# Weighing the values of two key tiles at a time, at the end of every second step, in a causal attention kernel

## The chip, the cores and the metric

The kernel runs on one core of one Trainium2 chip, in one launch. The metric is the device time in microseconds, the median of a few executions; lower is better. One further execution was taken by the hardware profiler, and all rows below come from that one.

## The reference, cut to what matters

The input `x` is 2 sequences of 2048 tokens with 256 channels. It is layer-normalised, then goes through a 16-head attention (16 channels a head) and, beside it, through a small gated feed-forward part; both results are added to `x`.

```python
att = jnp.einsum('bhqd,bhkd->bhqk', q, k) / np.sqrt(HEAD_DIM)
att = jnp.where(causal, att, 0.0)          # masked scores are 0, not -inf
att = jax.nn.softmax(att, axis=-1)
out = jnp.einsum('bhqk,bhkd->bhqd', att, v)
```

The masked scores are 0 and not minus infinity, so keys after the query keep a weight of exp(0 - row maximum) and their values have to be added in. The row maximum has to be known before the exponentials are taken.

## The kernel before, in words

A first stage (`stage_tokens`, the first 270 us or so) normalises the tokens, makes the projections, splits queries and keys into three bf16 parts each and writes them to HBM, together with the values and the feed-forward result. The second stage (`stage_attention`) is what the change touches.

**Groups, units, steps.** The 32 (sequence, head) pairs are handled as 8 groups of 4 heads. A group has 4 units `u` = 0 to 3, each of 512 queries. A unit goes through its key tiles `kt` of 128 keys, 4(u + 1) of them: 4, 8, 12 and 16 steps, 40 in a group and 320 in all. A step has 4 head steps. In each head step TensorE makes one score tile (`score_tile`, L1051: 128 keys x 512 queries, fewer queries in the last 4 tiles of a unit, which lie on the diagonal: 512, 384, 256, 128), and ScalarE takes its exponential into `probs` (L933). `ps_s` has room for 3 score tiles (`SRING`), so score tile n waits for the exponential of tile n - 3. `probs` has 16 slots, that is 4 key tiles; before its first exponential of key tile n ScalarE waits until key tile n - 4 is weighed (`probs_used`, L929). For diagonal tiles GpSimd then masks a 128 x 128 block of each head (L881).

**Pieces.** The row maxima are found beside this by computing the scores a second time in the other orientation: TensorE makes a piece (`score_piece`, L210: 128 queries x up to 512 keys) and VectorE reduces it to a row maximum (`reduce_piece`: L225 for a full piece, L221 with a mask for the piece on the diagonal, in two records, of which the second reads the accumulator). `ps_m` has room for 3 pieces (`MRING`), so piece n waits until VectorE is done with piece n - 3. The pieces are handed out by `SLOT_PIECES`: unit 0 issues 16 in 16 head steps, unit 1 issues 32 in 32, unit 2 issues 32 in its first 30 of 48 head steps and none after, and unit 3 issues 80 in 64, for the units of the next group. Head step 3 of each step of unit 3 has two. In the last group unit 3 has none; it makes output tiles instead (`output_tile`, L1097).

**Weighing.** `weigh_values` (L1065) multiplies the values of one key tile by the 4 heads' weights, in fp32, each head on its own 32 columns of the array: the profile shows 8 matmuls for the 4. This is called a quad below. In every step, after head step 2 and its pieces, the quad of the key tile two steps back (`LAG`) is issued. In steps 0 and 1 of a unit these are the last two key tiles of the unit before (`finish_unit`), and step 1 also adds the masked keys (`masked_keys`, L1075: 16 small matmuls, 32 in the profile), after which `ps_o` is complete (`out_ready`). That count releases ScalarE's copy of the sums (`keep_sums`, L920), GpSimd's next `spread_weight` (L848), and in unit 0 SyncE's loads for the next group (`load_group`). The quad of tile 0 waits until the copy is done (`sums_ready`).

**Other work on the same queues.** VectorE divides a finished unit in four small operations (`norm_step`, L968 to L979) in head steps 9 to 12 of the next unit, and makes the shift of a finished maximum (`max_step`) in six operations after the pieces. TensorE has suffix sums (`sum_suffix`, L1042 and L1043) at the end of steps 2, 4, 7 and 9 of unit 3 and turns a shift (`turn_shift`, L1028) at the end of steps 5 and 11 of unit 3, 2 of unit 1 and 8 of unit 2. Each engine runs its own instructions strictly in the order in which the program lists them; nothing is planned at run time. TensorE's order in a step is score, piece, score, piece, score, piece, quad, score, piece.

Of the kernel before, what the change touches and what calls it, by code (L numbers as in the profile page):

```python
# [18 lines left out]
NCH = T // CH  # L19
# [37 lines left out]
LAG = 2  # L57
# [23 lines left out]
def pieces_of(slot, head_step):  # L81

    lo, hi = SLOT_PIECES[slot]
    n, spread = hi - lo, SLOT_SPREAD[slot]
    at = min(head_step, spread)
    return range(lo + n * at // spread, lo + n * min(at + 1, spread) // spread)
# [10 lines left out]
def key_tiles(u):  # L97

    return SUB * (u + 1)


def first_query(u, kt):

    return P * max(0, kt - SUB * u)
# [600 lines left out]
def stage_attention(nc, ops, ident, ident16, attn_t, ffn_d, w_out_sb, out):  # L705
# [7 lines left out]
    with ExitStack() as ctx:  # L713
# [56 lines left out]
        def unit_of(i, p, u):  # L770

            return (i * 2 + p) * NCH + u
# [245 lines left out]
        def _(pe):  # L1018
            def turn_shift(u, n, quads):


                pe.wait_ge(shift_ready, n + 1)
                if not isinstance(n, int) or n > 0:
                    pe.wait_ge(shift_t_ready, n)
                if not isinstance(quads, int) or quads > 0:
                    pe.wait_ge(v_after_ready, quads)
                for s in range(SUB):
                    last = pe.transpose(ps_shift[0:3 * GH, s * P:(s + 1) * P],  # L1028
                                        shift[:, u, s].rearrange("p r h -> p (r h)"), ident16[:])
                last.then_inc(shift_turned, 1)  # L1030

            def sum_suffix(p, quad, n, turned_before):

                pe.wait_ge(after_ready, (n + 1) * (NT - 1))
                if not isinstance(n, int) or quad > 0:
                    pe.wait_ge(v_after_ready, n * 4 + quad)
                if not isinstance(turned_before, int) or turned_before > 0:
                    pe.wait_ge(shift_t_ready, turned_before)
                tiles = slice(quad * SUB, (quad + 1) * SUB)
                values = v_sb[:, p, tiles].rearrange("p s (h w) -> p (s h) w", w=HW)[:, :, 0:HD]  # L1040
                width = SUB * GH * HD
                pe.matmul(ps_x[:, 0:width], keys_after[:], values, start=True, stop=False)  # L1042
                pe.matmul(ps_x[:, 0:width], ones[:], after[:, tiles].rearrange("p s h d -> p (s h d)"),  # L1043
                          start=False, stop=True).then_inc(suffix_ready, 1)

            def score_tile(p, u, kt, h, G):

                slot = (KT0[u] + kt) * GH + h
                q0 = first_query(u, kt)
                pe.wait_ge(probs_ready, G * SLOTS + (slot + 1 if slot else SRING))  # L1050
                pe.matmul(ps_s[:, slot % SRING, 0:CH - q0], k_op[0:KROWS, p, h, kt * P:(kt + 1) * P],  # L1051
                          q_op[0:KROWS, p, h, u * CH + q0:(u + 1) * CH], start=True, stop=True).then_inc(scores_ready, 1)

            def weigh_values(p, u, kt, G):

                n = G * NCH + u
                if kt == 0:
                    pe.wait_ge(sums_ready, n + 1)
                if kt < SUB * u:
                    pe.wait_ge(probs_ready, G * SLOTS + (KT0[u] + kt + 1) * GH + SRING)  # L1060
                else:
                    pe.wait_ge(probs_masked, n * (SUB * GH) + (kt - SUB * u + 1) * GH)
                q0 = first_query(u, kt)
                for h in range(GH):
                    last = pe.matmul(ps_o[h * HW:(h + 1) * HW, q0:CH], v_sb[:, p, kt, h * HW:(h + 1) * HW],  # L1065
                                     probs[:, ((KT0[u] + kt) * GH + h) % PRING, 0:CH - q0], start=(kt == 0), stop=False)
                last.then_inc(probs_used, 1)

            def masked_keys(p, u, G):

                pe.wait_ge(diag_ready, G * NCH + u + 1)
                pe.wait_ge(v_after_ready, G * 4 + 4)
                for s in range(SUB):
                    for h in range(GH):
                        last = pe.matmul(ps_o[h * HW:(h + 1) * HW, s * P:(s + 1) * P],  # L1075
                                         v_after[:, p, u * SUB + s, h * HW:(h + 1) * HW],
                                         diag_weight[:, u % 2, h * SUB + s], start=False, stop=(s == SUB - 1))
                last.then_inc(out_ready, 1)

            def finish_unit(p, u, G, step):  # L1080

                weigh_values(p, u, key_tiles(u) - LAG + step, G)
                if step == LAG - 1:
                    masked_keys(p, u, G)

            def output_tile(k):


                n, t = divmod(k, SUB)
                b, c = divmod(n, NCH)  # L1090
                if k < MRING:
                    pe.wait_ge(ops.piece_reduced, B * NG * PIECES + MRING)
                else:
                    pe.wait_ge(total_ready, k + 1 - MRING)
                pe.wait_ge(normed_stored[c % 2], ((b + 1) * NG * (NCH // 2) - (NCH // 2 - 1 - c // 2) + 1) * STORES)
                for cc in range(CC):
                    last = pe.matmul(ps_m[:, k % MRING, 0:C], attn_t[:, b * CC + cc, c * CH + t * P:c * CH + (t + 1) * P],  # L1097
                                     w_out_sb[:, cc], start=(cc == 0), stop=(cc == CC - 1))
                last.then_inc(y_ready, 1)

            def group(i, p, first=False, last=False):
                G = i * 2 + p
                pe.wait_ge(q_loaded[p], (i + 1) * ops.LOADS)
                pe.wait_ge(k_loaded[p], (i + 1) * ops.LOADS)
                for u in range(NCH):
                    nxt = NCH if u == NCH - 1 else 0
                    pe.wait_ge(shift_loaded[u % 2], (G * (NCH // 2) + u // 2 + 2) * SHIFTS)
                    if nxt and not last:
                        pe.wait_ge(q_loaded[1 - p], (i + 1 + p) * ops.LOADS)
                        pe.wait_ge(k_loaded[1 - p], (i + 1 + p) * ops.LOADS)  # L1110
                    for kt in range(key_tiles(u)):
                        for h in range(GH):
                            score_tile(p, u, kt, h, G)
                            if not (nxt and last):
                                for f in pieces_of(u, kt * GH + h):
                                    ops.score_piece(pe, ps_m, MRING, f, 1 - p if nxt else p, (G + (nxt > 0)) * PIECES)
                            if h == 2:


                                if kt >= LAG:  # L1120
                                    weigh_values(p, u, kt - LAG, G)
                                elif u > 0:
                                    finish_unit(p, u - 1, G, kt)
                                elif not first:
                                    finish_unit(1 - p, NCH - 1, G - 1, kt)
                        if last and (u, kt) in OUT_AT:
                            output_tile(OUT_AT[u, kt])
                        if first and (u, kt) in FIRST_SV_AT:
                            sum_suffix(0, FIRST_SV_AT[u, kt], 0, 2)
                        if (u, kt) in SV_AT and not last:  # L1130
                            sum_suffix(1 - p, SV_AT[u, kt], G + 1,
                                       unit_of(i, p, NCH + sum(a == u and b < kt for a, b in SHIFT_AT)))
                        if (u, kt) in SHIFT_AT and not (nxt and last):
                            v = SHIFT_AT[u, kt]
                            quads = (G + 1) * 4 + (sum(b < kt for _, b in SV_AT) if nxt else 0)
                            turn_shift(v, unit_of(i, p, v + nxt), quads)
                if last:
                    for step in range(LAG):
                        finish_unit(p, NCH - 1, G, step)
                    for k in range(len(OUT_AT), OUTS):  # L1140
                        output_tile(k)

            for u in range(2):
                turn_shift(u, u, 0)
            group(0, 0, first=True)
            with pe.Fori(0, B * CC - 1) as i:
                group(i, 1)
                group(i + 1, 0)
# [29 lines left out]
```

## Time and profile before

| | us |
|---|---|
| median of 3 executions | 1267.76 (1265.9 to 1276.6) |
| the profiled execution | 1269.22 |
| its span (first to last instruction) | 1267.5 |
| TensorE busy | 1134.8 (90%) |
| VectorE busy | 962.7 (76%) |
| ScalarE busy | 743.7 (59%) |
| GpSimd busy | 361.1 (28%) |
| granted TensorE clock, mean | 0.969 of full |

TensorE's matmuls are pipelined: a matmul's duration is longer than its distance to the next one. So busy time says little of what the engine could still take, and the distances between start times in the timeline are read instead. "PEld" is the loading of TensorE's weights. A wait named in the profile is the idle time of an engine before an instruction, with the engine that released it.

### The profile page before, as it was taken

To read this page: it belongs to the slowest core of one execution; us is meant where nothing else is said; L and a number is where in the kernel's file an instruction comes from. 1 tells how busy PE (TensorE), PEld (TensorE's weight loads), DVE (VectorE), ACT (ScalarE), POOL (GpSimd) and SP (SyncE) were. 2 spreads that over 40 slices of the span, in tenths; PEclk is the share of its full clock that TensorE was granted. 3 is DMA by queue.
4 is the path that set the end of the run, shared out by engine and by line. 5 is a ranking of instruction groups with operands and counts; after the bars stand their busy time and mean duration, and the time that the engine had idled before them with its cause. 6 is when DMAs were issued, how large, how long until landed. Compare 5 with 4: busy or idle time off the path is not lost.

```text
span 1267.5 us, 26802 instructions
## 1 busy us (share of the span) xinstructions
PE 1134.8 (90%) x7168; PEld 470.0 (37%) x7168; DVE 962.7 (76%) x2433; ACT 743.7 (59%) x1553; POOL 361.1 (28%) x716
## 2 busy tenths in 40 slices
PE   2999388879998989998979999999899999999998
PEld 1666154533333323332333333333333333333345
DVE  5777388768689958895879689968696898689722
ACT  1554233236765766576647766676467667666773
POOL 6122011333314231323132313242223232314221
PEclk9999799979999989998989999999799999899999
DMA  2454953305400820091008200900090018002033
GB/s 91 140 176 144 152 186 116 99 19 69 75 5 6 96 49 6 6 104 42 5 8 96 51 4 7 142 7 3 6 122 27 2 25 124 6 2 76 6 97 112
DMA packets 59130, 79.57 MB, mean 63 GB/s; under 512 B 6112, under 2 KB 48480, under 8 KB 57952
## 3 DMA queue, kind: packets, MB, share of 16 engines
q1 hardware_dynamic: 57824, 73.56, 29.6%
q0 software_dynamic: 1152, 4.19, 1.1%
q8 instruction: 68, 1.11, 0.4%
q14 instruction: 86, 0.70, 0.2%
HBM read 43.78 MB, written 29.36 MB: 58 GB/s over the span
## 4 chain that ended last, share of the span: by engine, by line
PE 54%; issue 11%; DVE 9%; ACT 1%; POOL 1%; DVEq 1%; POOLq 0%; DMA 0%; SPq 0%; ACTq 0%
PE ps_o L1065 17%; PE ps_s L1051 16%; PE ps_m L210 15%; DVE part_max L225 3%; PE ps_o L1075 2%; PE ps_m L1097 2%; DVE ps_m L221 2%; ACT probs L933 1%; DVE row_max L238 1%; DVE part_max L221 1%; POOL after L202 1%; PE ps_x L1042 1%; PE ps_x L1043 1%; DVE turned L968 1%; PE ps_x L1028 1%
## 5 line engine op out<-in xcount | busy, mean ns | idle before, releaser
L933 ACT ACTIVATE probs<-ps_s 128x512 f32<-128x512 f32 (+3 forms) x1280 | 610.2, 535 | 309.1 <-PE ps_s L1051 304.4
L225 DVE TENSOR_REDUCE part_max<-ps_m 128x1 f32<-128x512 f32 x730 | 474.3, 681 | 37.8 <-PE ps_m L210 36.3
L1051 PE MATMUL ps_s<-q_op,k_op 99*128 99x512 bf16 (+3 forms) x1280 | 434.2, 358 | 16.8 <-issue 7.7
L210 PE MATMUL ps_m<-k_op,q_op 96*128 96x512 bf16 (+3 forms) x1200 | 405.3, 357 | 34.2 <-DVE part_max L225 24.4
L221 DVE CUSTOM_DVE_ANT_0 ps_m<-ps_m,mask 128x384 f32<-128x384 f32 x470 | 229.7, 497 | 136.4 <-PE ps_m L210 134.2
L1065 PE MATMUL ps_o<-probs,v_sb 128*32 128x512 f32 (+3 forms) x2560 | 306.0, 551 | 8.3 <-POOL probs L881 8.2
L881 POOL TENSOR_SCALAR_AFFINE_SELECT probs<-probs 128x128 f32<-128x128 f32 x512 | 143.2, 296 | 409.3 <-ACT probs L933 402.5
L1051 PEld LDWEIGHTS ps_s<-q_op,k_op 99*128 99x128 bf16 x1280 | 122.3, 98 | 337.3 <-ACT probs L933 222.1
L210 PEld LDWEIGHTS ps_m<-k_op,q_op 96*128 96x128 bf16 x1200 | 118.3, 99 | 191.6 <-DVE part_max L225 86.3
L848 POOL TENSOR_TENSOR diag_weight<-ident,masked_weight 128x2048 f32<-128x2048 f32 x32 | 115.5, 3610 | 123.8 <-ACT masked_weight L900 123.8
L1065 PEld LDWEIGHTS ps_o<-probs,v_sb 128*32 128x32 f32 x2560 | 51.1, 109 | 98.7 <-issue 41.7
L202 POOL TENSOR_TENSOR after<-after,v_sb 128x64 f32<-128x64 f32 x120 | 39.9, 333 | 139.2 <-DMA v_sb<-vpad_d 130.4
L221 DVE DVE_READ_ACCUMULATOR2_ANT part_max<- 128x1 f32 x512 | 71.8, 140 | 0.0
L631 PE MATMUL ps_qk<-xn_t,w_in_sb 128*128 128x512 f32 x128 | 60.3, 607 | 1.7 <-ACT xn_t L558 1.4
L210 PE MATMUL ps_pieces<-k_op,q_op 96*128 96x512 bf16 (+2 forms) x80 | 25.3, 354 | 35.1 <-DMA k_op<-parts_d 18.5
L402 POOL TENSOR_TENSOR k_act<-k_act 128x1024 f32<-128x1024 f32 x8 | 15.3, 1918 | 124.0 <-ACT k_act L596 124.0
L563 ACT ACTIVATE parts<-ps_qk 128x512 bf16<-128x512 f32 x32 | 19.0, 594 | 45.3 <-PE ps_qk L631 45.3
L407 POOL TENSOR_TENSOR ffn<-ffn,x_in 128x512 f32<-128x512 f32 x16 | 21.5, 1341 | 71.5 <-DVE ffn L486 71.5
L221 DVE CUSTOM_DVE_ANT_0 ps_pieces<-ps_pieces,mask 128x128 f32<-128x128 f32 (+3 forms) x42 | 20.1, 490 | 23.9 <-PE ps_pieces L210 23.6
L1075 PE MATMUL ps_o<-diag_weight,v_after 128*32 128x128 f32 x1024 | 37.1, 290 | 0.0
L568 ACT CAST parts<-rest 128x512 bf16<-128x512 f32 x32 | 19.7, 615 | 27.0 <-DVE rest L474 27.0
L620 PE MATMUL ps_xt<-ident,xn 128*128 128x128 f32 x64 | 9.4, 295 | 28.2 <-DVE xn L452 28.2
(84 smaller groups left out, 869.2 us busy)
## 6 DMA issues: line engine op xcount, KB each, us to landing
parts_d<-parts SPq DMA_DIRECT2D x48, 256.0 KB, 3.0
q_op<-parts_d SPq DMA_DIRECT2D x48, 256.0 KB, 14.9
k_op<-parts_d SPq DMA_DIRECT2D x48, 256.0 KB, 16.5
vpad_d<-v_pad SPq DMA_DIRECT2D x32, 256.0 KB, 3.2
v_sb<-vpad_d SPq DMA_DIRECT2D x8, 1024.0 KB, 26.6
x_in<-x SPq DMA_DIRECT2D x8, 512.0 KB, 4.9
ffn_d<-ffn SPq DMA_DIRECT2D x8, 512.0 KB, 3.2
attn_t<-normed SPq DMA_DIRECT2D x128, 32.0 KB, 2.3
```

The costliest lines, as they stand in the source:

```text
L202: pool.tensor_tensor(self.after[:, j], self.after[:, j + 1], values[:, j + 1, :, 0:HD], ALU.add).then_inc(self.after_ready, 1)
L210: last = pe.matmul(ps_m[:, f % ring, 0:width], self.q_op[0:ROWS, p, h, q0:q0 + P], self.k_op[0:ROWS, p, h, pc * CH:pc * CH + width], start ...
L221: dve.tensor_tensor_reduce(ps_m[:, f % ring, 0:width], ps_m[:, f % ring, 0:width], self.mask16[:, CH - width:CH], 1.0, LOWEST, ALU.add, AL ...
L225: dve.tensor_reduce(self.part_max[:, u % 2, h * SUB + s, pc:pc + 1], ps_m[:, f % ring, 0:width], AX_X, ALU.max).then_inc(self.piece_reduce ...
L631: last = pe.matmul(ps_qk[:, j % 2], w_in_sb[:, cc, j * P:(j + 1) * P], xn_t[:, cc, 1:CH + 1], start=(cc == 0), stop=(cc == CC - 1))
L848: pool.tensor_tensor(diag_weight[:, u % 2], ident[:].unsqueeze(1).broadcast_to([P, GH * SUB, P]), masked_weight[:, u].unsqueeze(2).broadca ...
L881: pool.affine_select(out=blk, in_=blk, compare_op=ALU.is_ge, fill=0.0, base=0, pattern=[[1, P]], channel_multiplier=-1).then_inc(probs_mas ...
L933: act.activation(probs[:, slot % PRING, 0:width], ps_s[:, slot % SRING, 0:width], ACT.Exp).then_inc(probs_ready, 1)
L1051: pe.matmul(ps_s[:, slot % SRING, 0:CH - q0], k_op[0:KROWS, p, h, kt * P:(kt + 1) * P], q_op[0:KROWS, p, h, u * CH + q0:(u + 1) * CH], sta ...
L1065: last = pe.matmul(ps_o[h * HW:(h + 1) * HW, q0:CH], v_sb[:, p, kt, h * HW:(h + 1) * HW], probs[:, ((KT0[u] + kt) * GH + h) % PRING, 0:CH ...
L1075: last = pe.matmul(ps_o[h * HW:(h + 1) * HW, s * P:(s + 1) * P], v_after[:, p, u * SUB + s, h * HW:(h + 1) * HW], diag_weight[:, u % 2, h ...
L1097: last = pe.matmul(ps_m[:, k % MRING, 0:C], attn_t[:, b * CC + cc, c * CH + t * P:c * CH + (t + 1) * P], w_out_sb[:, cc], start=(cc == 0), ...
```

## The change

The one call of `weigh_values` or `finish_unit` per step becomes two calls in every odd step and none in even ones, at the same place, after head step 2. In step `kt` (odd) it handles what steps `kt - 1` and `kt` handled. The quad of an even step so comes four head steps later, directly ahead of the other one; that of an odd step stays in its place. The last two quads of the whole program, after the last step, stay as they are.

```diff
                             if h == 2:


-                                if kt >= LAG:
-                                    weigh_values(p, u, kt - LAG, G)
-                                elif u > 0:
-                                    finish_unit(p, u - 1, G, kt)
-                                elif not first:
-                                    finish_unit(1 - p, NCH - 1, G - 1, kt)
+                                for step in range(kt - 1, kt + 1) if kt % 2 == 1 else ():
+                                    if step >= LAG:
+                                        weigh_values(p, u, step - LAG, G)
+                                    elif u > 0:
+                                        finish_unit(p, u - 1, G, step)
+                                    elif not first:
+                                        finish_unit(1 - p, NCH - 1, G - 1, step)
                         if last and (u, kt) in OUT_AT:
                             output_tile(OUT_AT[u, kt])
```

## Rows read from the trace of the kernel before

**Rows 1.** The page: TensorE and VectorE busy; the chain that ended last.
```profile
PE 1134.8 (90%) x7168; PEld 470.0 (37%) x7168; DVE 962.7 (76%) x2433; ACT 743.7 (59%) x1553; POOL 361.1 (28%) x716
...
PE 54%; issue 11%; DVE 9%; ACT 1%; POOL 1%; DVEq 1%; POOLq 0%; DMA 0%; SPq 0%; ACTq 0%
```

**Rows 2.** Stretches (start:end, length, engines' busy us, clock, DMA): units 0 to 3; last unit.
```profile
766.20:777.00 10.80, 10.31 (x98) 4.26 (x97) 9.97 (x24) 6.21 (x17) 4.62 (x16) 1.00 0.00 1
777.00:801.30 24.30, 22.14 (x165) 7.70 (x164) 22.82 (x53) 15.69 (x36) 8.08 (x17) 1.00 0.42 56
801.30:833.80 32.50, 30.08 (x213) 9.67 (x212) 22.53 (x53) 23.54 (x51) 12.28 (x32) 1.00 0.70 103
...
714.20:766.20 52.00, 50.48 (x330) 19.00 (x330) 44.70 (x137) 35.28 (x74) 11.91 (x19) 1.00 0.02 5
1206.60:1264.00 57.40, 56.38 (x385) 30.39 (x383) 15.90 (x37) 33.16 (x66) 11.22 (x22) 1.00 0.35 106
```

**Rows 3.** Timeline: start, duration, engine, line, operation; around one full quad.
```profile
807.50 0.38 PE L1051 MATMUL ps_s<-q_op,k_op 99*128 99x512 bf16 x1
...
807.72 0.38 PE L210 MATMUL ps_m<-k_op,q_op 96*128 96x512 bf16 x1
...
808.02 1.06 PE L1065 MATMUL ps_o<-probs,v_sb 128*32 128x512 f32 x8
...
809.02 0.10 PEld L1051 LDWEIGHTS ps_s<-q_op,k_op 99*128 99x128 bf16 x1 [0.84 <-ACT probs L933]
809.02 0.39 PE L1051 MATMUL ps_s<-q_op,k_op 99*128 99x512 bf16 x1
...
809.25 0.10 PEld L1051 LDWEIGHTS ps_s<-q_op,k_op 99*128 99x128 bf16 x1
809.41 0.38 PE L1051 MATMUL ps_s<-q_op,k_op 99*128 99x512 bf16 x1
```

**Rows 4.** Timeline: a 128-query quad with the masked keys right behind it.
```profile
805.05 0.42 PE L1065 MATMUL ps_o<-probs,v_sb 128*32 128x128 f32 x8
805.29 1.06 PE L1075 MATMUL ps_o<-diag_weight,v_after 128*32 128x128 f32 x32
806.28 0.39 PE L1051 MATMUL ps_s<-q_op,k_op 99*128 99x512 bf16 x1
```

**Rows 5.** Timeline: last piece before a quad; VectorE behind it.
```profile
797.28 0.39 PE L210 MATMUL ps_m<-k_op,q_op 96*128 96x512 bf16 x1
...
797.09 1.88 DVE L225 TENSOR_REDUCE part_max<-ps_m 128x1 f32<-128x512 f32 x3
799.24 0.57 DVE L221 CUSTOM_DVE_ANT_0 ps_m<-ps_m,mask 128x384 f32<-128x384 f32 x1 [0.27 <-PE ps_m L210]
...
799.72 1.88 DVE L225 TENSOR_REDUCE part_max<-ps_m 128x1 f32<-128x512 f32 x3
```

**Rows 6.** Groups of VectorE in unit 3 (714.2 to 766.2): pieces; a transpose of the division.
```profile
L225 DVE TENSOR_REDUCE part_max<-ps_m 128x1 f32<-128x512 f32 x37 | 24.8, 685 | 2.5 <-PE ps_m L210 2.3
L221 DVE CUSTOM_DVE_ANT_0 ps_m<-ps_m,mask 128x128 f32<-128x128 f32 (+3 forms) x42 | 20.2, 494 | 12.3 <-PE ps_m L210 12.1
...
L979 DVE STREAM_TRANSPOSE normed<-turned 128x512 f32<-128x512 f32 x1 | 0.7, 711 | 0.1
```

**Rows 7.** VectorE's waits in unit 2 (801.3 to 833.8): us, times, longest.
```profile
DVE part_max L225 <- PE ps_m L210: 1.2, 3, 0.5
DVE ps_m L221 <- PE ps_m L210: 0.8, 1, 0.8
```

**Rows 8.** TensorE's own waits over the attention (271 to 1206).
```profile
PE ps_m L210 <- DVE part_max L225: 24.4, 44, 1.5
PE ps_o L1065 <- POOL probs L881: 8.2, 6, 2.3
...
PE ps_m L210 <- DVE part_max L221: 5.9, 21, 0.4
```

**Rows 9.** Timeline: GpSimd's masks late in unit 2.
```profile
829.98 2.76 POOL L881 TENSOR_SCALAR_AFFINE_SELECT probs<-probs 128x128 f32<-128x128 f32 x11
```

## The prediction

> **What bounds the kernel now.** I read the page first [rows 1]: TensorE is busy 90% and holds 54% of the chain that ended last, VectorE 9%. That alone would say that whatever shortens TensorE's work shortens the kernel. The split by units corrects it [rows 2]. VectorE is busy 9.97 of 10.80 us in unit 0 (92%) and 22.82 of 24.30 in unit 1 (94%); in unit 3 it is 44.70 of 52.00 (86%), beside TensorE's 50.48. In unit 2 there are no pieces in the last 18 head steps, and no engine is full. So two engines run close together: VectorE sets the pace in units 0, 1 and the first part of 2, TensorE in unit 3. They are coupled by three buffers of pieces, and TensorE's own waits show the coupling: 24.4 + 5.9 us in 65 places behind a reduction [rows 8]. ScalarE is busy 15.69 of 24.30 and 35.28 of 52.00 [rows 2] and has slack.
>
> What matters then is how long TensorE stays away from the pieces in one go, against how much work three pieces are for VectorE. The timelines give both.
>
> **What the pair saves on TensorE.** Score and piece follow each other at 0.22 us (807.50, 807.72) [rows 3]. From the piece to the quad it is 0.30, that is 0.08 more, and from the quad to the next score 1.00. In a run of such matmuls the rate is better [rows 4]: the 32 masked-key matmuls are 8 waves of 128 queries and take 1.06 us to the end of the last. Less the about 0.29 us that one such matmul lasts by itself (taken from 0.42 for a short quad of two waves, less one wave) that is 0.77 for 7 distances, 0.11 a wave. A full quad is 8 such waves, 0.88 us; so leaving the mode costs 1.00 - 0.88 = 0.12 us and entering it 0.08. A merged pair takes 1.96 instead of 2 x 1.08 = 2.16 us: 0.20 us saved, in 159 pairs (of 160, the last one is merged already) 32 us of TensorE time. No matmul and no weight load goes; the whole gain is the switch.
>
> Where the 0.12 comes from shows in the weight loads: in the steady rhythm the next score's weights are loaded at 809.25, 0.16 us ahead of its matmul at 809.41; behind the quad load and matmul both start at 809.02 [rows 3]. The Trainium skill, "TensorE: Matmul & The Clock Gate", step "LDWEIGHTS — get the stationary operand into the array", says that the queue pulls weight loads ahead of matmuls in flight; by that rule alone leaving the mode would cost nothing, and the saving would be 0.08 a pair, 13 us in all. The trace doesn't agree at this place, and the sum goes by the row.
>
> **What the pair costs VectorE.** Now the time from the start of the last piece ahead of a quad to the start of the next reduction: 797.28 to 799.24, 1.96 us [rows 5]. The merged pair puts 0.88 us more in between: 2.84 us. When that piece is issued, the one three back has just been released, so VectorE has at most three pieces to do. Three full ones take 1.88 to the end of the last, about 0.61 each [rows 5]. In unit 3 the mix is lighter [rows 6]: 37 full ones at 0.61, and 42 diagonal ones of 0.494 on average, of which each holds up the next by 0.09 less than that (799.24 to 799.72 for one of 0.57 [rows 5]): (37 x 0.61 + 42 x 0.40) / 79 = 0.50 each. Full buffers are thus 1.8 us of work in units 0 to 2 and 1.5 in unit 3. **They cover a lone quad almost (1.96) and a pair not (2.84)**: VectorE will stand still 1.05 us a pair in units 0 to 2 and 1.3 us in unit 3. This is a price per pair, with these exceptions:
> - step 1 has the masked keys behind a 128-query quad now, to which a 256-query one is added: only 0.44 us more. I take 0.9 us idle there (1.2 in unit 3, where the buffers hold less; from 0.8 for the largest wait at such a place [rows 7] plus 0.44, with a little off for fuller buffers).
> - in step 3 the division's 0.7 us transpose [rows 6] is done at head step 12, between the buffered pieces: 0.35 and 0.6 instead of 1.05 and 1.3.
>
> **The sum, by units of one group.** Idle now is the stretch less VectorE's busy time [rows 2].
> - Unit 0, 2 pairs: 0.9 + 0.35 = 1.25, now 0.83: +0.45.
> - Unit 1, 4 pairs: 0.9 + 0.35 + 2 x 1.05 = 3.35, now 1.48: +1.85.
> - Unit 2: up to the pair in step 7, behind which there are no pieces, 0.9 + 0.35 + 1.05 = 2.3, now 2.0 [rows 7]: +0.3. That pair itself +0.88. The two in steps 9 and 11 fall into the tail without pieces, with short diagonal tiles, where TensorE gains: -0.4. There the quad of tile 8 waits for its mask now, 8.2 us in 6 places over the run [rows 8]; it moves four head steps later, but comes then with tile 9's, whose mask is among the 11 that end at 832.74 [rows 9]. Of the at most 1.1 us a group I take half: -0.5. Together +0.3.
> - Unit 3, 8 pairs: 1.2 + 0.6 + 6 x 1.3 = 9.6, and 0.5 for the suffix sums that come right behind the pair of steps 7 and 9; now 7.3: +2.8. (TensorE's saving is used up here: VectorE's 44.7 + 10.1 = 54.8 us is above TensorE's 52.0 - 1.6.)
>
> That is +5.4 us a group, for 7 groups 38. The last group has units 0 to 2, +2.6, and a unit 3 without pieces, in which TensorE is busy all the time [rows 2]. It gains 0.2 a pair, 1.6, if ScalarE can follow; with three score buffers and about 0.55 us an exponential (35.28 us of ScalarE for 64 of them and a few copies [rows 2]) the score behind the even step has to wait some 0.35 us a pair, which makes it +1.2. I take 0. Sum: **+40 us**.
>
> **Waits that move.** The quad of tile n frees `probs` slots. ScalarE needs tile n - 4 weighed: for an even n that is the first quad of the pair in step n - 1, which TensorE issues ahead of that step's last score. ScalarE must wait for that score anyway, so no wait is added; cost nothing, hidden by that order. The wait for `sums_ready` moves a step later and only gets easier. `out_ready` comes 0.44 us later: the copy of the sums, GpSimd's spreading and SyncE's loads start that much later; no DMA is moved past another, and these have a whole unit of slack. What ScalarE loses in a pair (three scores, 1.65 us, against the same 2.84) it has in slack. The clock: mean granted 1.00 in most units [rows 2]; TensorE gets no longer pauses than now, so I cost it at nothing; where it runs at its lower level (1.2 GHz) a pair is twice as long, which is part of the upper end.
>
> The Trainium skill's "TensorEngine Tiling (Array Packing)", "Performance Considerations", speaks against the change in the same way: packing speeds up TensorE but not the emptying of PSUM, which may then become the bottleneck. It names no price; with the 32 us saved alone the run would be at 1237, and the rows above say why it isn't.
>
> **Bounds.** From below: all 32 us come through and the 8.2 us of mask waits go: -40, 1229. From above: each of 20 pairs in a group costs VectorE the full 0.88, less the half of the idle time (11.6 us a group by the figures above) that belongs to quads of even steps: 17.6 - 5.8 = 11.8 a group, 94 for 8: 1363.
>
> **Rivals.**
> 1. **It gets faster, the switch decides.** TensorE sets the pace everywhere, and VectorE catches up between pairs: between two pairs TensorE has 8 head steps. For it: 54% of the chain, and 50.48 of 52.00 in unit 3. Against: VectorE needs 5.6 us of every 6.5 in unit 3 and 22.82 of 24.30 in unit 1, so the idle 1.05 to 1.3 us can't be made up. It decides if VectorE's idle time a pair stays under about 0.9 us in unit 3. Time: 1229 to 1250, 1240. Chance 0.14.
> 2. **It cancels.** The buffers are fuller at the pair than now (TensorE waits more for VectorE, so VectorE has always three ahead, and suffix sums and shift turns in even steps are covered) and unit 3 gains 1 us a group rather than losing 2.8: +13 or less, 1255 to 1280. Chance 0.12.
> 3. **It costs more.** VectorE's standing still is passed on in full, as in the upper bound, and ScalarE's scores run dry too: 1330 to 1363, 1345. For it: rows 5 show 0.27 idle already behind a lone quad. Chance 0.18.
> That the change doesn't do what it says is not a separate case: the order is fixed in the program.
>
> **How the numbers follow.** The forecast has 0.56. Its time is 1269.2 + 40 = 1309 for a run like the profiled one, which was 1.5 us above the median; so 1308. The range goes from 1258 (the rest of rival 2 and the unknown half of the mask waits) to 1345 (the middle of rival 3). 1% is 12.7 us and about what a measurement of this kernel tells from no change. Faster 0.14, same 0.12, slower 0.74.
>
> **What would show it.** In the profile after: pair to next score 1.9 us after the pair's start (16 matmuls in one row of the timeline); VectorE waiting for L210 about once every two steps, 1.0 to 1.3 us each, with the sum of its waits well over today's; unit 1 about 26 us, unit 3 about 55, unit 2 nearly unchanged; `L1065 <- POOL` smaller; no ScalarE wait for a quad. Wrong it would be if unit 3 came out at 52 or less with VectorE's waits behind a pair under 0.9 us.

## The result, and the profile after

The changed kernel takes 1331.53 us (median of 4, 1328.7 to 1333.05), the kernel before 1266.83 beside it: 1.054 times as long, interval 1.047 to 1.060, some 65 us. The forecast was 1308 and slower, in a range of 1258 to 1345. The profiled execution took 1328.7 us with a span of 1326.9, 59.4 more than the span before.

The page of the changed kernel: span, busy time, the chain that ended last.

```profile
span 1326.9 us, 26802 instructions
...
PE 1168.5 (88%) x7168; PEld 501.1 (38%) x7168; DVE 960.8 (72%) x2433; ACT 732.2 (55%) x1553; POOL 363.1 (27%) x716
...
PE 54%; DVE 14%; issue 7%; ACT 2%; DVEq 1%; ACTq 0%; DMA 0%; SPq 0%
```

The instruction counts are those of before and VectorE's busy time is the same, but its share of the chain went from 9% to 14% [rows 1]. The work did not grow; the waiting did.

Stretches of the changed kernel: start:end, length, then busy time (and instructions) of TensorE, its weight loads, VectorE, ScalarE, GpSimd, the granted clock, DMA. The first four are units 0 to 3 (unit 0 of an earlier group than the others), the last is the last unit up to the end of the output tiles.

```profile
528.90:540.80 11.90, 10.62 (x98) 4.70 (x98) 10.77 (x26) 6.34 (x17) 4.58 (x16) 1.00 0.01 2
1069.80:1098.40 28.60, 24.90 (x165) 9.57 (x164) 23.05 (x51) 15.55 (x35) 8.20 (x17) 0.88 0.43 56
1098.40:1131.70 33.30, 31.11 (x213) 10.77 (x212) 21.97 (x52) 23.07 (x51) 12.66 (x32) 1.00 0.60 93
1131.70:1187.50 55.80, 53.18 (x333) 20.57 (x331) 44.19 (x137) 34.47 (x74) 11.86 (x18) 0.97 0.02 4
1264.00:1322.00 58.00, 54.93 (x382) 30.90 (x381) 15.10 (x35) 32.40 (x66) 11.20 (x22) 1.00 0.34 102
```

Against [rows 2]: unit 0 went from 10.8 to 11.9 us, unit 1 from 24.3 to 28.6, unit 2 from 32.5 to 33.3, unit 3 from 52.0 to 55.8. The stretches of before all ran at full clock, while the 28.6 us hold 6.8 us at the lower clock and the 55.8 us hold 3.4; so not the whole difference is the pair's own (more on this behind the first experiment). In unit 1 VectorE is now busy 23.05 of 28.60 us, where it was busy 22.82 of 24.30. Over all groups, from first score to first score of the units (sums of the start times in each trace, us):

| | before | after | difference | forecast | spread in 4: before | spread in 4: after |
|---|---|---|---|---|---|---|
| unit 0, 8 times | 93.4 | 108.2 | +14.8 | +3.6 | 92.9 | 113.9 |
| unit 1, 8 times | 199.5 | 224.2 | +24.7 | +14.8 | 190.8 | 201.2 |
| unit 2, 8 times | 266.2 | 268.4 | +2.2 | +2.4 | 260.9 | 270.6 |
| unit 3, 7 times | 376.2 | 390.9 | +14.7 | +19.6 | 372.4 | 386.5 |
| last unit to the end | 60.8 | 62.9 | +2.1 | 0 | 60.8 | 62.9 |
| lower clock within the span, us | 79 | 120 | +41 | none | 58 | 90 |

The first 271 us account for the remaining 1.0. (The last two columns are experiments of the next section.) That unit 2 came out at its forecast is in part chance: in the trace before 10.0 us of its 266.2 were at the lower clock, after none. Its stretches at full clock went from 32.5 to 33.3 us in three groups and by 1.8 and 1.9 in two others.

Around a pair in unit 3, in the timeline of the changed kernel:

```profile
892.87 0.34 PE L210 MATMUL ps_m<-k_op,q_op 96*128 96x384 bf16 x1
893.07 0.14 DVE L221 DVE_READ_ACCUMULATOR2_ANT part_max<- 128x1 f32 x1
893.07 0.69 DVE L225 TENSOR_REDUCE part_max<-ps_m 128x1 f32<-128x512 f32 x1
893.14 0.16 PEld L1065 LDWEIGHTS ps_o<-probs,v_sb 128*32 128x32 f32 x8 [0.17 <-issue]
893.14 1.92 PE L1065 MATMUL ps_o<-probs,v_sb 128*32 128x512 f32 x16
...
893.67 0.56 DVE L221 CUSTOM_DVE_ANT_0 ps_m<-ps_m,mask 128x384 f32<-128x384 f32 x1
...
895.00 0.39 PE L1051 MATMUL ps_s<-q_op,k_op 99*128 99x512 bf16 x1
...
895.22 0.60 PE L210 MATMUL ps_m<-k_op,q_op 96*128 96x512 bf16 x2
...
895.64 0.69 DVE L225 TENSOR_REDUCE part_max<-ps_m 128x1 f32<-128x512 f32 x1 [1.35 <-PE ps_m L210]
```

From the pair to the next score it is 1.86 us, where two lone quads took 1.00 each [rows 3]: the saving of TensorE is there, as worked out. And VectorE, with what it had left, is done 1.35 us before the next piece can be reduced. In unit 1 the same thing reads 1.25:

```profile
827.29 1.88 DVE L225 TENSOR_REDUCE part_max<-ps_m 128x1 f32<-128x512 f32 x3
...
827.61 0.38 PE L210 MATMUL ps_m<-k_op,q_op 96*128 96x512 bf16 x1
...
827.92 1.92 PE L1065 MATMUL ps_o<-probs,v_sb 128*32 128x512 f32 x16
...
830.42 0.43 DVE L221 CUSTOM_DVE_ANT_0 ps_m<-ps_m,mask 128x256 f32<-128x256 f32 x1 [1.25 <-PE ps_m L210]
```

Other pairs show the same. VectorE's longest wait behind a pair at full clock, as the middle value over the groups, is 1.2 us in step 1 of unit 3, 0.2 in step 3, and 1.6, 1.35, 0.9, 1.2 and 1.4 in steps 5 to 13; in steps 3, 5 and 7 of unit 1 it is 0.4, 1.25 and 0.9.

In the rows of unit 1 three full pieces, 1.88 us, are reduced back to back, and they are over at 829.17, while TensorE's pair lasts until about 829.8 (827.92 + 1.92). Then TensorE has to wait for VectorE, which is behind. TensorE's own waits in the attention:

```profile
PE ps_m L210 <- DVE part_max L225: 42.9, 80, 2.5
...
PE ps_m L210 <- DVE part_max L221: 9.1, 31, 0.7
```

They were 24.4 and 5.9 us [rows 8]. The 8.2 us behind GpSimd's masks that stood beside them is gone. So the change made each engine wait for the other in turn.

**What the forecast did not have.** Once a group, at the start of unit 1, VectorE stands behind GpSimd. The timeline of the changed kernel there:

```profile
807.43 3.61 POOL L848 TENSOR_TENSOR diag_weight<-ident,masked_weight 128x2048 f32<-128x2048 f32 x1
...
808.63 2.44 DVE L238 TENSOR_TENSOR row_max<-raw_max,floor 128x16 f32<-128x16 f32 x1
...
811.73 0.61 PE L210 MATMUL ps_m<-k_op,q_op 96*128 96x512 bf16 x1 [2.47 <-DVE part_max L225]
...
813.98 1.51 PE L1065 MATMUL ps_o<-probs,v_sb 128*32 128x256 f32 x16
815.26 1.94 PE L1075 MATMUL ps_o<-diag_weight,v_after 128*32 128x128 f32 x32
...
818.14 0.43 DVE L221 CUSTOM_DVE_ANT_0 ps_m<-ps_m,mask 128x256 f32<-128x256 f32 x1 [3.36 <-PE ps_m L210]
```

L238 compares 16 numbers a partition with a floor; elsewhere it takes 0.15 to 0.17 us (2.21 in the first group, in both kernels). Here it takes 2.44 and ends at 811.07, when GpSimd's spread ends (811.04). The same rows of the kernel before:

```profile
777.68 3.61 POOL L848 TENSOR_TENSOR diag_weight<-ident,masked_weight 128x2048 f32<-128x2048 f32 x1
...
779.72 1.60 DVE L238 TENSOR_TENSOR row_max<-raw_max,floor 128x16 f32<-128x16 f32 x1
```

There L238 began 2.04 us into the spread, now 1.20, and stays 0.84 us longer. The Trainium skill, "SBUF — State Buffer", section "Who interferes with whom", says that a VectorE instruction with two inputs in SBUF contends with a GpSimd instruction that reads SBUF, that the shared ports are an exclusive lock, and that the order of issue decides who blocks; the trace agrees, with 2.44 us for the one that began second. TensorE then waits 2.47 us for a free buffer (1.42 at this place before), and from 811.00 on, within that pause, its clock is down. Three stretches of unit 1 of that group (columns as above):

```profile
806.80:811.00 4.20, 2.22 (x10) 0.73 (x8) 4.11 (x7) 2.87 (x6) 3.83 (x2) 1.00 0.16 35
811.00:817.80 6.80, 6.07 (x56) 3.14 (x57) 3.71 (x12) 1.22 (x3) 0.04 (x1) 0.50 0.00 0
817.80:835.50 17.70, 16.82 (x102) 5.74 (x101) 15.17 (x34) 11.43 (x28) 4.34 (x15) 1.00 0.65 82
```

In the middle one the granted clock is 0.50, the lower level of 1.2 GHz, and into it fall the pair of step 1 and the masked keys: 3.15 us from 813.98 to the next score at 817.13. So VectorE waits 3.36 us there, and not 0.9.

### The profile page after: what moved, and what is told of

The parts are those of the page before. It is cut to its first block, busy times and chain, and to the rows that moved or that the text cites. A ratio compares the mean times of both kernels' runs of the same rounds, so it can differ in the third digit from the quotient of the medians.

```text
span 1326.9 us, 26802 instructions
## 1 busy us (share of the span) xinstructions
PE 1168.5 (88%) x7168; PEld 501.1 (38%) x7168; DVE 960.8 (72%) x2433; ACT 732.2 (55%) x1553; POOL 363.1 (27%) x716
## 4 chain that ended last, share of the span: by engine, by line
PE 54%; DVE 14%; issue 7%; ACT 2%; DVEq 1%; ACTq 0%; DMA 0%; SPq 0%
PE ps_o L1065 20%; PE ps_m L210 15%; PE ps_s L1051 13%; DVE part_max L225 6%; PE ps_o L1075 3%; DVE ps_m L221 3%; PE ps_m L1097 2%; ACT probs L933 2%; DVE row_max L238 2%; DVE part_max L221 1%; DVE turned L968 1%; PE ps_x L1042 1%; PE ps_x L1043 1%; DVEq L217 1%; PE ps_x L1028 1%
## 5 line engine op out<-in xcount | busy, mean ns | idle before, releaser
L933 ACT ACTIVATE probs<-ps_s 128x512 f32<-128x512 f32 (+3 forms) x1280 | 599.5, 542 | 372.4 <-PE ps_s L1051 368.2
L210 PE MATMUL ps_m<-k_op,q_op 96*128 96x512 bf16 (+3 forms) x1200 | 419.7, 360 | 65.0 <-DVE part_max L225 42.9
L1065 PE MATMUL ps_o<-probs,v_sb 128*32 128x512 f32 (+3 forms) x2560 | 282.6, 562 | 0.0
L848 POOL TENSOR_TENSOR diag_weight<-ident,masked_weight 128x2048 f32<-128x2048 f32 x32 | 115.4, 3608 | 125.0 <-ACT masked_weight L900 125.0
L1065 PEld LDWEIGHTS ps_o<-probs,v_sb 128*32 128x32 f32 x2560 | 69.8, 114 | 132.7 <-issue 77.2
L1075 PE MATMUL ps_o<-diag_weight,v_after 128*32 128x128 f32 x1024 | 41.9, 314 | 0.0
L1075 PEld LDWEIGHTS ps_o<-diag_weight,v_after 128*32 128x32 f32 x1024 | 35.2, 129 | 1.0
L631 PEld LDWEIGHTS ps_qk<-xn_t,w_in_sb 128*128 128x128 f32 x128 | 24.3, 195 | 26.5 <-issue 22.2
```

Of the source, the lines that this page charges most:

```text
L210: last = pe.matmul(ps_m[:, f % ring, 0:width], self.q_op[0:ROWS, p, h, q0:q0 + P], self.k_op[0:ROWS, p, h, pc * CH:pc * CH + width], start ...
L631: last = pe.matmul(ps_qk[:, j % 2], w_in_sb[:, cc, j * P:(j + 1) * P], xn_t[:, cc, 1:CH + 1], start=(cc == 0), stop=(cc == CC - 1))
L848: pool.tensor_tensor(diag_weight[:, u % 2], ident[:].unsqueeze(1).broadcast_to([P, GH * SUB, P]), masked_weight[:, u].unsqueeze(2).broadca ...
L933: act.activation(probs[:, slot % PRING, 0:width], ps_s[:, slot % SRING, 0:width], ACT.Exp).then_inc(probs_ready, 1)
```

## The experiments

Theory 1: three buffered pieces don't cover the time of a pair, and VectorE starves. Theory 2: the stall behind GpSimd and the lower clock behind it are most of the loss. All times are medians, beside runs of the kernel before on the same chip: 1264.89 for the spread in four parts, the piece between and the pair in unit 3; 1272.25 for the cheap reductions and the other buffers; 1267.01 for the pair in units 0 and 1 and for the last experiment.

### GpSimd's spread in four parts, in both kernels

```diff
-                pool.tensor_tensor(diag_weight[:, u % 2], ident[:].unsqueeze(1).broadcast_to([P, GH * SUB, P]),
-                                   masked_weight[:, u].unsqueeze(2).broadcast_to([P, GH * SUB, P]),
-                                   ALU.mult).then_inc(diag_ready, 1)
+                for q in range(4):
+                    part = slice(q * SUB, (q + 1) * SUB)
+                    pool.tensor_tensor(diag_weight[:, u % 2, part], ident[:].unsqueeze(1).broadcast_to([P, SUB, P]),
+                                       masked_weight[:, u, part].unsqueeze(2).broadcast_to([P, SUB, P]),
+                                       ALU.mult).then_inc(diag_ready, 1)
...
-                pe.wait_ge(diag_ready, G * NCH + u + 1)
+                pe.wait_ge(diag_ready, (G * NCH + u + 1) * 4)
```

On the changed kernel:

> The changed kernel with GpSimd's spread of the masked weights (3.6 us in one instruction) cut into four instructions of a quarter each. In the changed kernel one small VectorE operation of the shift (L238) takes 2.44 us once a group where it ends exactly with that spread, 1.60 before. Theory 1 (three buffered pieces don't cover the pair): only this stall and the pauses behind it go, at most 2.3 us a group and part of the lower clock behind it: 1305 to 1325, unit 2 and unit 3 unchanged at 33.3 and 55.8 us. Theory 2 (the stall behind GpSimd and the lower clock that follows are most of the loss): below 1290.

On the kernel before:

> The kernel before with the same cut of the spread into four. Both theories: the 1.60 us stall of each group shrinks to at most 0.9, so 1 to 1.5 us a group: 1250 to 1262. If the sum over a group doesn't move, VectorE makes the time up elsewhere: 1267.

Measured: changed 1308.63 (1303.24 to 1310.16; ratio 1.033, 1.026 to 1.040), before 1253.77 (ratio 0.991, 0.988 to 0.995). The stall shrinks to a part of the spread (changed kernel with the cut, timeline; its lines behind the edit stand two lower, so L848 is L850 and L1065 is L1067):

```profile
799.70 4.03 POOL L850 TENSOR_TENSOR diag_weight<-ident,masked_weight 128x512 f32<-128x512 f32 x4
...
800.90 0.87 DVE L238 TENSOR_TENSOR row_max<-raw_max,floor 128x16 f32<-128x16 f32 x1
```

Without the long stall the distance is still 1308.6 - 1253.8 = 55 us of the 65. Theory 2 falls as the main cause. It has a share: the cut brings the changed kernel 23 us and the kernel before 11, so 10 to 12 us of the 65 come from the longer stall and what follows it. In the table unit 1 shows it: the loss there is 24.7 us with the long spread and 10.4 with the short one, while unit 3 loses 14.7 and 14.1. "Unit 2 and unit 3 unchanged" held for unit 2 (33.3 in four of eight groups, up to 0.9 more in three) and roughly for unit 3 (54.3 for 55.8; the 55.8 held 3.4 us at the lower clock). But unit 0 got longer, 13.5 us in most groups instead of 11.9, and its loss in the table went from 14.8 to 21.0. Its granted clock is 0.87 there:

```profile
1045.00:1058.50 13.50, 12.22 (x98) 4.90 (x98) 11.03 (x26) 6.38 (x17) 4.61 (x16) 0.87 0.02 5
```

The lower clock moved from one unit to another. Why it falls in just these places was not settled.

What the pair costs by itself is read from stretches that have neither the lower clock nor the long stall. Unit 3 and unit 1 of one group, with the spread cut, of the kernel before and of the changed one (columns as above):

```profile
952.10:1004.10 52.00, 50.49 (x330) 19.01 (x330) 44.72 (x137) 35.27 (x74) 12.80 (x25) 1.00 0.02 5
1014.90:1038.90 24.00, 22.09 (x165) 7.71 (x164) 22.53 (x53) 15.66 (x35) 8.52 (x20) 1.00 0.42 57
```

```profile
990.60:1045.00 54.40, 51.71 (x334) 20.33 (x330) 44.05 (x137) 34.64 (x74) 12.70 (x24) 1.00 0.02 5
1058.50:1083.60 25.10, 22.50 (x166) 8.48 (x165) 21.73 (x50) 15.56 (x36) 8.60 (x20) 1.00 0.47 59
```

VectorE's idle time (length less busy) went from 7.3 to 10.35 us in unit 3 and from 1.5 to 3.4 in unit 1; the forecast had 10.1 and 3.35. The lengths grew by 2.4 and 1.1 us. Unit 0 at full clock grew by 1.1 and unit 2 by about 1.3. That is 5.9 us a group, where the forecast has 5.4. Over the run, with the last unit's 2.1, it makes about 47 us, an estimate from these stretches. The other 18 or so of the 65 are left for the longer stall and the lower clock. At half the clock TensorE does at least half the work, so 41 us more of it can cost at most 21 us.

### A piece between the two quads

```diff
-                            if not (nxt and last):
+                            if not (nxt and last) and not (kt % 2 == 1 and h == 3):
                                 for f in pieces_of(u, kt * GH + h):
                                     ops.score_piece(...)
...
+                                    if step == kt - 1 and not (nxt and last):
+                                        for f in pieces_of(u, kt * GH + 3):
+                                            ops.score_piece(...)
```

> The changed kernel, still both quads in the odd step, but the piece or two pieces of head step 3 are issued between the two quads and no longer behind them. The switch is paid twice again (0.20 us a pair lost), ScalarE's gap without scores gets longer still, VectorE's gap without pieces falls to about what it was before the change. Theory 1: most of the loss comes back, 1270 to 1290. Theory 2, or if ScalarE's gap were what costs: 1320 or more.

Measured: 1332.7 (1328.33 to 1340.09), no better than the change itself. The expectation was wrong, and by its own words 1320 or more speaks for theory 2 or for ScalarE's gap as the cost. The trace has another reading. TensorE and VectorE around such a pair in unit 1:

```profile
833.58 0.38 PE L210 MATMUL ps_m<-k_op,q_op 96*128 96x512 bf16 x1
833.89 1.06 PE L1065 MATMUL ps_o<-probs,v_sb 128*32 128x512 f32 x8
834.89 0.28 PE L210 MATMUL ps_m<-k_op,q_op 96*128 96x256 bf16 x1
835.10 1.06 PE L1065 MATMUL ps_o<-probs,v_sb 128*32 128x512 f32 x8
836.10 0.45 PE L1051 MATMUL ps_s<-q_op,k_op 99*128 99x384 bf16 x2
836.38 0.38 PE L210 MATMUL ps_m<-k_op,q_op 96*128 96x512 bf16 x1
```

```profile
835.36 0.43 DVE L221 CUSTOM_DVE_ANT_0 ps_m<-ps_m,mask 128x256 f32<-128x256 f32 x1 [0.24 <-PE ps_m L210]
...
836.80 0.69 DVE L225 TENSOR_REDUCE part_max<-ps_m 128x1 f32<-128x512 f32 x1 [0.95 <-PE ps_m L210]
```

I had counted one gap and not two. The piece that goes between is taken from behind the pair, where two scores now come before the next one. From 833.58 to 836.38 it is 2.80 us for one more piece, which here is a short one; VectorE stands 0.24 + 0.95 = 1.19 us in place of 1.25, and TensorE pays the switch twice. The long stall is there too, 3.05 us in this kernel. In unit 3 the reading can be checked without stall and lower clock:

```profile
1011.00:1066.90 55.90, 52.92 (x330) 19.21 (x330) 45.66 (x138) 33.55 (x74) 11.84 (x18) 1.00 0.02 4
```

VectorE is idle 10.2 us there, no less than the 10.35 with the pair in one piece. The unit takes 1.5 us more than the 54.40 above; 8 pairs at 0.20 us of switch would be 1.6. So the piece between took nothing from VectorE's idle time, and the added time fits a saving that is given back. That what counts is the work that VectorE gets in the whole stretch in which quads are made, and not the longest single gap, fits this; no run tests it by itself. ScalarE's gap as the cost is left to the next experiments.

### The pair in some units only

The same edit in both, with `u == 3` or `u < 2`:

```diff
-                                for step in range(kt - 1, kt + 1) if kt % 2 == 1 else ():
+                                for step in ((range(kt - 1, kt + 1) if kt % 2 == 1 else ()) if (u == 3) else (kt,)):
```

> The pair only in steps of unit 3 (issued there: the last two tiles of unit 2 and tiles 0 to 13 of unit 3), one quad a step elsewhere. Theory 1 with the sizes of the trace after (unit 3 from 52 to 55 or 56 us in 7 groups, +2 in the last): 1280 to 1292. Theory 2: units 0 and 1, where the stall is, are as before: 1265 to 1272.

> The pair only in steps of units 0 and 1, one quad a step elsewhere. With the sizes of the trace after (unit 0 from 10.8 to 11.9, unit 1 from 24.3 to 27.7 or 28.6 where the stall behind GpSimd and the lower clock come with it): +30 to +42 us, 1297 to 1310. Theory 2, in which the lower clock comes from the sum of all pauses: less, under 1290.

Measured: unit 3 alone 1285.86 (ratio 1.016, 1.009 to 1.023), as theory 1 had it; units 0 and 1 alone 1290.34 (1.021, 1.017 to 1.025), 7 us under the range given and at the limit named for theory 2. In the traces unit 3 alone lengthens the unit 3s from 376.2 to 390.3 and the last unit by 2.1; units 0 and 1 alone lengthen those from 292.9 to 323.8, 31 us, which is in the expected size, but units 2 and 3 were 12.7 us shorter than in the trace before. The expectation added the units to one trace before, which held more of the lower clock in units 2 and 3 than this one. 21.0 + 23.3 = 44 us of the 65 are thus placed. Pairs in unit 2 cost 9.7 us in the two kernels with the cut spread (table), not 2.4; the remaining 11 or so are not placed.

### Cheap reductions

VectorE reduces 128 columns of each piece only, so the maxima are those of a part of the keys.

```diff
-            dve.tensor_tensor_reduce(ps_m[:, f % ring, 0:width], ps_m[:, f % ring, 0:width],
-                                     self.mask16[:, CH - width:CH], ...
+            dve.tensor_tensor_reduce(ps_m[:, f % ring, width - P:width], ps_m[:, f % ring, width - P:width],
+                                     self.mask16[:, CH - P:CH], ...
...
-        dve.tensor_reduce(..., ps_m[:, f % ring, 0:width], ...
+        dve.tensor_reduce(..., ps_m[:, f % ring, 0:P], ...
```

> The kernel before, in which VectorE reduces only 128 columns of each piece (the row maxima are then those of a part of the keys); TensorE makes the pieces in full. VectorE is far from a bound. Both theories: TensorE sets the pace, its 24.4 + 5.9 us of waits go and the stall behind GpSimd has slack: 1215 to 1250.

> The changed kernel with the same cheap reductions. Three buffers of pieces can't starve an engine that has time to make up for it. Theory 1: the 0.20 us of switch a pair shows, 15 to 32 us less than the kernel before with cheap reductions. Rival (ScalarE's missing scores or the order of the quads cost time by themselves): the changed one is as slow or slower than the other, also with cheap reductions.

Measured: 1223.83 (1208.01 to 1225.72) for the kernel before with it, 1211.26 (1207.51 to 1212.79) for the changed one. The 65 us of loss are gone: the changed kernel is 12.6 us faster by the medians, a little under the 15 to 32 expected. That it is faster is not beyond doubt, since the ranges overlap (one run of the kernel before took 1208.01). Unit 3 of one group in both (columns as above; before, then changed):

```profile
1045.20:1096.10 50.90, 50.88 (x330) 19.40 (x329) 26.28 (x138) 35.26 (x74) 11.77 (x18) 0.95 0.02 5
```

```profile
1028.60:1078.30 49.70, 49.28 (x329) 20.59 (x329) 26.41 (x137) 34.12 (x74) 12.02 (x19) 0.98 0.02 5
```

VectorE is busy half the time and TensorE nearly all of it. Over the run the unit 3s gain 10.6 us and the unit 2s 12.6; units 0 and 1 lose 8.4 and the last unit 2.1. The unit 3s do not show the saving of 0.20 us a pair, though: 24.6 us of them were at the lower clock in the kernel before and 3.3 in the changed one, and 21.3 us less at half the clock are worth up to 10.7. (The two rows above hold 4.7 and 1.8 us of it.) TensorE's waits for ScalarE's exponentials also rose, from 7.9 to 17.7 us. Of the unit 2s' gain most is the wait for masks, beside 14.4 us less at the lower clock (below, of the kernel before, then of the changed one, both with cheap reductions).

```profile
PE ps_o L1065 <- POOL probs L881: 16.4, 7, 3.2
```

```profile
PE ps_o L1065 <- POOL probs L881: 5.3, 7, 1.3
```

So VectorE's load decides whether the pair costs anything; the scores that ScalarE misses and the order of the quads cost no such sum by themselves. L238 stands 3.24 us behind the spread in both of these kernels, so they say nothing about that stall. That units 0 and 1 don't gain even here is open.

### Four buffers of pieces, two of scores

```diff
-SRING = 3
-MRING = 3
+SRING = 2
+MRING = 4
```

> The kernel before with 4 buffers of pieces and 2 of scores (3 and 3 now; PSUM is full). VectorE gets 2.4 us of cover in place of 1.8, ScalarE 1.1 in place of 1.65. I expect ScalarE's side to cost as much as VectorE's gives: 1255 to 1290.

> The changed kernel with 4 buffers of pieces and 2 of scores. Theory 1: VectorE's standing still behind a pair falls from 1.25 to about 0.65 us in unit 1 and from 1.35 to 0.85 in unit 3, so the distance to the kernel before with the same buffers falls from 65 to 15 to 45 us, as long as ScalarE keeps its slack. If ScalarE's gap is what costs, the distance grows beyond 65.

Measured: 1321.11 for the kernel before with it (1318.68 to 1322.3, far above the 1255 to 1290 expected: two score buffers cost more than a fourth piece buffer gives), 1353.6 for the changed one. The distance is 32.5 us (24.4 between the two traces), half of the 65, inside the range of theory 1. Unit 2 of one group in the kernel before with these buffers, then of two groups in the changed one:

```profile
1083.90:1118.80 34.90, 31.76 (x213) 9.65 (x212) 22.82 (x53) 24.64 (x51) 12.70 (x32) 1.00 0.59 91
```

```profile
705.10:740.20 35.10, 31.72 (x214) 10.74 (x213) 22.05 (x52) 24.62 (x51) 12.74 (x32) 1.00 0.58 89
1101.10:1140.20 39.10, 34.90 (x214) 11.14 (x213) 22.18 (x52) 24.63 (x51) 12.74 (x32) 0.92 0.54 81
```

In units 0, 1 and 3 the pair now costs almost nothing: 94.3 to 96.4, 208.1 to 211.4 and 388.5 to 391.3 us in sum, 8 us where it was 54. In unit 2 it costs 20.7 (282.8 to 303.5; it was 2.2). That comes with the lower clock: 39.4 us of the changed kernel's unit 2s are at it and none of the other's, and the two unit 2s without it take 35.1 and 38.1 us, where the same groups took 35.0 and 37.9. Why the clock falls there is open.

It looks as if the fourth buffer covered the pair, but VectorE's waits say otherwise. The expectation had them fall to 0.65 us in unit 1 and 0.85 in unit 3; measured as above they are 1.3 in step 5 of unit 1, and 1.75, 1.5, 1.0, 1.1 and 1.1 in steps 5 to 13 of unit 3. Unit 3 of one group, of the kernel before with these buffers, then of the changed one:

```profile
991.55:1045.93 54.38, 51.99 (x329) 18.94 (x329) 44.84 (x135) 36.48 (x74) 11.80 (x19) 1.00 0.02 5
```

```profile
1008.01:1062.95 54.94, 51.94 (x331) 20.32 (x330) 44.55 (x137) 36.10 (x74) 11.86 (x18) 1.00 0.02 4
```

With the pair VectorE is idle 10.4 us, as with three buffers. What moved is the kernel before: with two score buffers it has 9.5 us of idle time in VectorE and 54.38 us of length already, where it had 7.3 and 52.00. By this reading the distance fell because little was left to lose. The run speaks against ScalarE's gap as the cost, with which the distance should have grown beyond 65; it is no proof of theory 1.

### The pair only where no pieces are made

Steps 9 and 11 of unit 2, with the spread in four parts; the condition of the edit above becomes `u == 2 and kt >= 8`.

> The kernel before with GpSimd's spread in four parts, once more, as the standard for the next one: 1250 to 1258.

> The kernel before with the spread in four parts, and the pair only in steps 9 and 11 of unit 2, where no pieces are made. Theory 1: nothing starves there, 0.2 us a pair and the wait of tile 8's quad for its mask (8.2 us in 6 places before) are won: 4 to 14 us under the kernel with the spread alone, 1240 to 1250. If delayed quads cost something by themselves: no gain or a loss.

Measured: 1249.2 (1246.73 to 1250.76; ratio to the kernel before 0.988, 0.985 to 0.991), against 1255.01 (1248.76 to 1264.28; 0.991, 0.988 to 0.995) for the spread alone. TensorE's wait for masks in the kernel with the spread alone

```profile
PE ps_o L1067 <- POOL probs L883: 8.8, 7, 2.1
```

is not among its waits in the other: it is gone. 5.8 us between the medians fit that, but the two intervals overlap, so only the gain of both edits together, 1.2%, is beyond doubt. It is the fastest kernel here that takes the row maxima over all keys.

## Why the prediction was right, and where its sizes were off

**What bounds the kernel.** The reading that TensorE's 54% of the chain misleads, and that VectorE's three buffers decide, held. With cheap reductions the loss is gone, and VectorE's idle time came where and nearly as large as worked out. The other division of the buffers doesn't prove it, though its distance fell: VectorE's waits did not.

**The saving on TensorE**, 0.20 us a pair: 1.86 us from the pair to the next score, where 1.88 was worked out, and the 1.5 us by which a unit 3 grew when a piece came between the quads of its 8 pairs fit it. In the sums of the cheap kernels it does not stand out from the lower clock. The rule of the Trainium skill ("TensorE: Matmul & The Clock Gate", the step on LDWEIGHTS), weight loads pulled ahead, would have given 0.08; the row decided rightly. The missing lead goes with the splitting of the array's columns and not with the type fp32: in the trace before, behind the fp32 suffix sums on all 128 columns (L1043), the next score's load starts at 747.60, 0.21 us ahead of its matmul at 747.81.

**VectorE's idle time a pair**, 1.3 in unit 3 and 1.05 in units 0 to 2: 0.9 to 1.6 in steps 5 to 13 of unit 3, 1.3 on average, and 1.25 and 0.9 in steps 5 and 7 of unit 1. Of the exceptions, step 1 of unit 3 was 1.2 as forecast, and step 3 was 0.4 in unit 1 (forecast 0.35) and 0.2 in unit 3 (forecast 0.6). Unit 3 was forecast at +19.6 and came at +14.7. The last unit, taken as 0 between -1.6 and +1.2, was +2.1, outside these bounds. The reason named, ScalarE's three score buffers, is there: TensorE waits 2.5 us in 8 places for exponentials, none before. That alone would make +0.9; the rest is open.

**The term that was mis-sized is unit 1**, +1.85 us a group, measured +3.1 on average over the 8, and unit 0 beside it, +0.45, measured +1.1 in a quiet group (10.8 to 11.9) and +1.85 on average. Without the long stall and the lower clock the forecast's own terms come out well in sum, 5.9 us a group for 5.4, though not one by one: unit 1 is then +1.1 and not +1.85, unit 3 +2.4 and not +2.8, unit 0 +1.1 and not +0.45, unit 2 about +1.3 and not +0.3. VectorE's idle time came as forecast in units 1 and 3; the lengths did not follow it to the letter, since VectorE's busy time within a unit changed too (10.77 us for 9.97 in unit 0, 21.73 for 22.53 in unit 1), which looks like work moved over the border between them. Two parts of the excess were costed at nothing. The first: a VectorE operation that already stood 1.60 us behind GpSimd's spread. It was in the list of the chain as L238, and its start hangs on the order of events that the change shifts. The second: the clock, which I costed at nothing because TensorE would get no longer pauses. At this place it did, 2.47 us for 1.42, and the time at the lower level went from 79 to 120 us. How much of the 65 the clock is by itself no run isolates; it is at most 21, and the longer stall and what follows it are 10 to 12, some of which is that same clock.

**The waits called free** were free: ScalarE has no wait for a quad in the trace after, and the mask waits went, by 8.2 us instead of the half that I took.

**The rivals.** "It gets faster" is ruled out by the time; the cheap kernels show that the loss goes when VectorE has slack, and leave open whether a gain comes. "It cancels" is ruled out. "It costs more" began at 1330 and the median is 1331.5, so the size lies at its lower edge; but not by its mechanism, VectorE's idle time passed on in full everywhere: unit 3 passed on less than forecast, and unit 1 had an added stall. That the median lies in the range owes to its upper end, which was taken from this rival.

## What to carry to other kernels

When work is batched to save an engine a switch, compare the length of the batch with what its consumers have buffered, not with their busy share: here 2.84 us without a new piece against three buffers of 1.5 to 1.8 us turned a true saving of 0.20 us a pair into a loss of some 47 us, and the whole change, with what it set off besides, into one of 5%. Batch only where no such consumer is fed. And before a move in time is called free, look in the chain of waits for short operations with long durations: here one stood behind another engine, and the move changed for how long. And compare lengths only between stretches with the same granted clock: here unit 2 seemed unchanged and the cheap kernels seemed to gain in unit 3 by differences that the clock covers.

## What was not expected of the hardware

A VectorE operation on 16 numbers a partition, 0.15 to 0.17 us elsewhere, took 2.44 and 3.05 us beside a 3.61 us GpSimd instruction, and ended with it each time. Cutting GpSimd's instruction into four of about 1.04 us cut the stall to 0.87 and gained the kernel before 11 us.

TensorE's granted clock fell to 0.50 within a pause of 2.47 us and stayed there for 6.8 us. The total time at that level differed between kernels that do the same work: 56 us in the last one above, 120 in the changed kernel.
